# Scatter of expert outputs in tiles of 128 tokens across batch borders, with the expert outputs read back in two parts

## The reference

```python
def _L0_ffn_ref(x, gate_w, gate_b, w1, w2):
    E, H, K = 32, 2048, 8
    logits = einsum('bsd,ed->bse', x, gate_w) + gate_b
    probs = softmax(logits, axis=-2)                    # over the tokens
    vals, idx = top_k of probs per expert, K tokens     # (b, K, E)
    merged = einsum('bked,bke->bed', x[idx], vals)      # one row per batch and expert
    h = gelu(einsum('bei,eih->beh', [merged, 1], w1))
    o = einsum('bej,ejo->beo', [h, 1], w2)              # one row of 512 per batch and expert
    out = zeros_like(x).at[b, idx].add(o * vals)        # scatter back to the picked tokens

x = x + _L0_attn_ref(_layernorm(x), ...)
x = x + _L0_xattn_ref(_layernorm(x), ctx_512, ...)
x = x + _L0_ffn_ref(_layernorm(x), ...)
```

## Time and profile before

| What | Value |
|---|---|
| Median of 3 runs | 2419.74 us (2414.06 to 2422.43) |
| The profiled execution's own time | 2416.22 us |
| Its span in the trace | 2414.6 us |
| PE busy | 1965.3 us, 81% of the span |
| DVE, ACT, POOL busy | 974.0, 753.5 and 826.0 us |
| HBM read, written | 306.39 MB, 16.15 MB |

### The profile page before, as it was taken

The page is one execution under the profiler, slowest core; times in us unless marked ns, Lnnn a source line. Parts: engine busy times, 40 slices in busy tenths (PEclk is TensorE's granted clock), DMA queues, the critical chain, the costliest instruction groups (busy, mean ns, idle before and its releaser), DMA issues. The chain is left out here.

```text
span 2414.6 us, 39997 instructions
## 1 busy us (share of the span) xinstructions
PE 1965.3 (81%) x11970; PEld 1156.2 (48%) x11970; DVE 974.0 (40%) x2477; ACT 753.5 (31%) x1551; POOL 826.0 (34%) x592
## 2 busy tenths in 40 slices
PE   7789999999999999999999999986765565565533
PEld 5465666666666666666666666653211111111101
DVE  1354655656556555465555565642100000000003
ACT  2143434435444444344443444433100000000000
POOL 0244555545455455545454554553000000000000
PEclk9899999999999999999999999987877777778765
DMA  5233223233232332422323324263799999999974
GB/s 156 59 77 94 73 78 86 72 98 75 70 91 69 80 84 70 102 56 76 85 75 93 75 70 98 65 212 137 314 419 423 420 419 422 421 422 420 420 238 134
DMA packets 135414, 419.34 MB, mean 174 GB/s; under 512 B 32612, under 2 KB 74820, under 8 KB 110804
## 3 DMA queue, kind: packets, MB, share of 16 engines
q1 hardware_dynamic: 130292, 410.08, 50.0%
q10 hardware_dynamic: 4096, 7.80, 1.0%
q0 software_dynamic: 992, 1.02, 0.1%
HBM read 306.39 MB, written 16.15 MB: 134 GB/s over the span
## 5 line engine op out<-in xcount | busy, mean ns | idle before, releaser
L1035 DVE TENSOR_REDUCE maxes<-bank 112x1 f32<-112x376 f32 (+1 forms) x1024 | 508.4, 537 | 221.2 <-PE bank L1240 220.6
L863 ACT ACTIVATE probs<-bank 125x448 f32<-125x448 f32 x768 | 400.8, 546 | 355.5 <-PE bank L1262 350.1
L1262 PE MATMUL bank<-q_st,k_st 98*125 98x224 f32 x1536 | 388.0, 343 | 10.1 <-DMA q_st<-max_lo 5.5
L739 POOL TENSOR_TENSOR psum_keys<-psum_keys,probs 125x896 f32<-125x896 f32 x128 | 268.8, 2100 | 300.2 <-ACT probs L863 290.7
L1600 PE MATMUL bank<-ring,hid_T 128*32 128x512 f32 x1024 | 179.3, 864 | 207.6 <-DMA ring<-in_L_ffn_w 202.7
L1240 PE MATMUL bank<-k_st,q_st 96*112 96x376 f32 (+1 forms) x1024 | 324.1, 371 | 16.1 <-DVE maxes L1035 7.6
L1262 PEld LDWEIGHTS bank<-q_st,k_st 98*125 98x125 f32 x1536 | 270.9, 195 | 120.0 <-issue 71.5
L742 POOL TENSOR_TENSOR psum_keys<-psum_keys,probs 125x896 f32<-125x896 f32 x128 | 267.3, 2088 | 10.0
L1515 DVE TENSOR_TENSOR o_fin<-bank,b_row 16x512 f32<-16x512 f32 x32 | 21.7, 679 | 591.3 <-PE bank L1558 591.3
L1438 POOL DMA_DIRECT2D o_rows<-o_fin x31 | 15.3, 492 | 597.7 <-DVE o_fin L1515 597.7
L1240 PEld LDWEIGHTS bank<-k_st,q_st 96*112 96x112 f32 x1024 | 166.8, 183 | 75.2 <-DVE maxes L1035 39.3
(11 more groups left out here) (149 smaller groups left out, 2271.1 us busy)
## 6 DMA issues: line engine op xcount, KB each, us to landing
ring<-in_L_ffn_w SPq DMA_DIRECT2D x128, 2048.0 KB, 30.7
k_st<-k_hi SPq DMA_DIRECT2D x512, 93.8 KB, 2.2
k_st<-k_lo SPq DMA_DIRECT2D x256, 93.8 KB, 2.2
q_st<-q_hi SPq DMA_DIRECT2D x512, 28.0 KB, 1.8
ctx_nat<-in_ctx SPq DMA_DIRECT2D x16, 750.0 KB
x_in<-in_x SPq DMA_DIRECT2D x16, 448.0 KB, 3.5
q_st<-q_lo SPq DMA_DIRECT2D x256, 28.0 KB, 1.9
out<-x SPq DMA_DIRECT2D x16, 448.0 KB, 7.5
```

What stands on the lines that cost most here:

```text
L739: nc.gpsimd.tensor_tensor(psum_keys[:], psum_keys[:], lo, ALU.add).then_inc(pool_chain, 1)
L863: nc.scalar.activation(probs[n % 2][:, j, :], bank[5 + u % 2][0:SK, 0:2 * T], ACT.Exp, scale=SCALE).then_inc(probs_ready, 1)
L1035: nc.vector.tensor_reduce(maxes[:, j, t, c:c + 1], bank[2 + n % 3][0:TT, 0:SC[c + 1] - SC[c]], AX.X, ALU.max).then_inc(s_drained, 1)
L1262: last = nc.tensor.matmul(bank[5 + u % 2][0:SK, kk * T:(kk + 1) * T], k_st[slot][:, j, k * SK:(k + 1) * SK], q_st[slot][:, j, :], start=Tr ...
```

## The change

Three edits, all in the third part.

1. The x of all 3584 tokens is handled as 28 tiles of 128 consecutive tokens, whatever batch they are in. They are loaded by four DMAs of 8, 8, 8 and 4 tiles (a partition gets one token's 2 KiB of each tile), and stored one tile at a time, 28 stores of 128 partitions with 2 KiB each.
2. Four batches are seven tiles, so the scatter runs in four cycles of seven tiles. A tile that lies over a batch border gets its PSUM bank from the matmuls of two batches, each for its own partitions; a piece that doesn't fit the array's column groups of 32, 64 or 128 is split in two. This gives 12 matmuls in a cycle. VectorE takes the tiles in the order 0, 2, 4, 6, 1, 3, 5.
3. The expert rows are read back in two parts: experts 0 to 15 by four DMAs ahead of the loads of x, experts 16 to 30 by four DMAs where all were read before.

```diff
-        def fin(b):
-            return ring[0:TT, b // RW, b % RW * 2 * D:(b % RW + 1) * 2 * D].rearrange(
-                "p (t n) -> p t n", t=2)
+        NT = B * T // P
+        PER = 2 * H // D
+        rows_out = out.rearrange("b t d -> (b t) d").rearrange("(k p) d -> p k d", p=P)
+        def fin(k):
+            return ring[:, k // PER, k % PER * D:(k % PER + 1) * D]
+        CYCLE = RW * T // P
+        TURN = [0, 2, 4, 6, 1, 3, 5]
+        def drained(k):
+            return k // CYCLE * CYCLE + TURN.index(k % CYCLE) + 1
+        def tile_at(n):
+            return n // CYCLE * CYCLE + TURN[n % CYCLE]
...
                 weights(end, 1, False, (0, 1))
-                for b in range(B):
-                    if b % RW == 0:
-                        sp.wait_ge(h_full if b < B // 2 else o_full, E - 1)
-                    sp.dma_start(fin(b), out[b, :, :].rearrange("(p t) d -> p t d", p=TT)
-                                 ).then_inc(fin_loaded[b // RW], 16)
+                def read_back(r, e0, e1):
+                    sp.dma_start(o_in[r * E + e0:r * E + e1, :, :],
+                                 o_rows.rearrange("(g r) e n -> r e g n", r=RW)[r, e0:e1, :, :]
+                                 ).then_inc(o_loaded, 16)
+                sp.wait_ge(o_stored, 16 * (E - 4))
+                for r in range(RW):
+                    read_back(r, 0, E // 2)
+                for g in range(-(-NT // PER)):
+                    sp.wait_ge(h_full if g < 2 else o_full, E - 1)
+                    n = min(PER, NT - g * PER)
+                    sp.dma_start(ring[:, g, 0:n * D].rearrange("p (k d) -> p k d", d=D),
+                                 rows_out[:, g * PER:g * PER + n, :]).then_inc(fin_loaded[g], 16)
                 weights(end, 1, False, (2, 3))
                 sp.wait_ge(o_stored, 16 * (E - 1))
                 for r in range(RW):
-                    sp.dma_start(o_in[r * E:(r + 1) * E - 1, :, :],
-                                 o_rows.rearrange("(g r) e n -> r e g n", r=RW)[r, 0:E - 1, :, :]
-                                 ).then_inc(o_loaded, 16)
+                    read_back(r, E // 2, E - 1)
...
-                for b in range(B):
-                    act.wait_ge(fin_ready, 2 * b + 2)
-                    act.dma_start(out[b, :, :].rearrange("(p t) d -> p t d", p=TT), fin(b)
-                                  ).then_inc(fin_stored, 16)
-                act.wait_ge(fin_stored, 16 * B)
+                for n in range(NT):
+                    k = tile_at(n)
+                    act.wait_ge(fin_ready, n + 1)
+                    act.dma_start(rows_out[:, k, :], fin(k)).then_inc(fin_stored, 16)
+                act.wait_ge(fin_stored, 16 * NT)
...
-                for b in range(B):
-                    g, r = b // RW, b % RW
-                    if r == 0:
-                        dve.wait_ge(fin_loaded[g], 16 * RW)
-                    for t in range(2):
-                        dve.wait_ge(scat_full, g * 2 * RW + t * RW + r + 1)
-                        nc.vector.tensor_tensor(fin(b)[:, t, :], fin(b)[:, t, :],
-                                                bank[t * RW + r][0:TT, :], ALU.add
-                                                ).then_inc(fin_ready, 1)
+                for n in range(NT):
+                    k = tile_at(n)
+                    dve.wait_ge(fin_loaded[k // PER], 16)
+                    dve.wait_ge(scat_full, n + 1)
+                    nc.vector.tensor_tensor(fin(k), fin(k), bank[k % 8][:], ALU.add
+                                            ).then_inc(fin_ready, 1)
...
-                pe.wait_ge(o_loaded, 16 * (RW + GB))
-                for g in range(GB):
-                    for t in range(2):
-                        for r in range(RW):
-                            if g:
-                                pe.wait_ge(fin_ready, (g - 1) * 2 * RW + 2 * r + t + 1)
-                            rows = slice(r * E, (r + 1) * E)
-                            nc.tensor.matmul(bank[t * RW + r][0:TT, :],
-                                             tokens(picks[rows, g, :], t), o_in[rows, g, :],
-                                             start=True, stop=True).then_inc(scat_full, 1)
+                pe.wait_ge(o_loaded, 16 * (2 * RW + GB))
+                def scatter(k, r, first, parts, new, done):
+                    k += cycle * CYCLE
+                    if new and k >= 8:
+                        pe.wait_ge(fin_ready, drained(k - 8))
+                    rows = slice(r * E, (r + 1) * E)
+                    for at, n in parts:
+                        last = nc.tensor.matmul(bank[k % 8][at:at + n, :],
+                                                picks[rows, cycle, first:first + n],
+                                                o_in[rows, cycle, :], start=True, stop=True)
+                        first += n
+                    if done:
+                        last.then_inc(scat_full, 1)
+                for cycle in range(GB):
+                    scatter(0, 0, 0, [(0, 128)], True, True)
+                    scatter(1, 1, 0, [(96, 32)], True, False)
+                    scatter(3, 2, 0, [(64, 64)], True, False)
+                    scatter(5, 3, 0, [(32, 32), (64, 64)], True, False)
+                    scatter(2, 1, 32, [(0, 128)], True, True)
+                    scatter(4, 2, 64, [(0, 128)], True, True)
+                    scatter(6, 3, 96, [(0, 128)], True, True)
+                    scatter(1, 0, 128, [(0, 64), (64, 32)], False, True)
+                    scatter(3, 1, 160, [(0, 64)], False, True)
+                    scatter(5, 2, 192, [(0, 32)], False, True)
```

## The result

The changed kernel takes 2434.44 us (median of 4 runs, 2431.54 to 2438.99) against 2418.9 us for the kernel before: a ratio of 1.0063, 95% interval 1.0041 to 1.0085. It is slower by about 15 us, where 40 us less were forecast. The profiled execution took 2431.54 us.

The account below looks back on a forecast made before the run. The last 110 us were taken as the place to gain: loads of x, a read-back on one DMA engine, then the scatter. -8.9 + 3.0 - 29.6 - 4 = -39.5 us from 2418.5 gave 2379 us, range 2368 to 2392.

Parts of the forecast that it names:

- D: Scatter's start to the span's end: 26.7 us instead of 30.4, about -4 us, bounds -1 to -6.5.
- TensorE at half clock with VectorE waiting for it in each cycle (D gone): Sign in the changed profile's scatter that would show the forecast wrong, with the gain of D lost; no size given.
- A: Loads of x as four DMAs of 128 partitions: 372 GB/s instead of 257, -8.9 us, bounds 0 to -11.5.
- B: Read-back's first part (16 experts, 0.524 MB) ahead of the loads of x: costs its whole time, +3.0 us.
- C: From the last w2 to the scatter's start: 11.8 us instead of 41.4, -29.6 us.
- What bounds the kernel: Last 110 us: loads of x and w2 pure transfer, then the read-back on one engine, then VectorE and stores about level.
- the engine counts: DMA transfers: partitions shared out evenly among up to 16 engines, so 31 get 1, 16 get 16, 15 get 15.
- hidden either way: Read-back's second part (0.49 MB) right behind w2: 1.3 us or 4.1, within the 7.8 us before expert 31's rows.
- Transfers on one engine: Rival: both read-back parts stay on one DMA engine, 2407 us (2389 if only the second does); 5 in 100.
- cost by the piece: Rival: loads, stores and read-back cost by count of pieces, not bytes; sum +26 us, 2444 us; 4 in 100.
- the fixed part of a store: Rival: the scatter's 28 stores each pay 1.7 us fixed in turn; sum +9 us, 2428 us; 2 in 100.

Follow-up runs that it names:

- e1: The changed kernel with the 12 matmuls of a cycle put in order of width, VectorE's order changed to match: 2382.47 us, ratio to before 0.987.
- e2: The changed kernel in its own order, with every matmul cut into pieces of 32 columns: 2381.01 us, ratio 0.985.
- e8: The kernel of e1 with the matmuls of a cycle in pairs of one width (128, 64, 32, 128, 64, 32): 2403.82 us, ratio 0.9965.
- e4: The changed kernel with the old read-back (31 experts at once, behind the last weights): 2452.88 us, ratio 1.0145.
- e9: The kernel of e1 with SP waiting, ahead of the read-back's second part, until the last expert's w2 chunks have landed: 2371.79 us, ratio 0.9842.
- e5: The kernel of e1 with the read-back's first part (experts 0 to 15) moved behind the last weights: 2369.62 us, ratio 0.9848.

## Why the prediction was wrong

The step that failed is D, the scatter, and in it one clause: "Each row group has three per cycle, evenly, so the same packing can hold." I took 0.435 us a matmul from a stretch in which all were 32 x 112, four abreast, and multiplied it by 48 matmuls of three widths. The diff's order mixes the widths, and then they don't go abreast: from its start to the end of the span the scatter takes 2429.9 - 2350.79 = 79.1 us, where 26.7 were forecast and 30.4 measured before. e1, e2 and e8 show that the width changes are the cause. The Trainium skill ("TensorEngine Tiling (Array Packing)", Key Properties) states a rule that fits: switching the tiling mode, as against the tile, drains TensorE. The traces agree, 1.84 to 2.0 us for each group between two changes. I had not weighed that rule, and none of my rivals was this one; the closest sign I named was "TensorE at half clock with VectorE waiting for it in each cycle (D gone)", and I gave it no price. The rest of the sum holds up: sorted by width (e1), the kernel takes 2382.47 us, inside the range of 2368 to 2392, though partly because A's error and D's make up for B's. (The middle of 2416.2 and 2419.7 is 2418.0, not 2418.5; that changes nothing.)

With that, the difference of the two profiled executions adds up from intervals of before, after and e4:

| Term | Forecast, us | Measured, us | From |
|---|---|---|---|
| Before this stretch | 0 | -1.5 | expert 30's w2 stage, 2290.88 against 2292.41 |
| A, loads of 128 partitions | -8.9 | -11.4 | e4's interval against before's |
| B, narrow read-back and the stream | +3.0 | +9.1 | the interval after against e4's |
| C, last w2 to scatter | -29.6 | -29.5 | 11.9 against 41.4 |
| D, scatter to the end | -4 | +48.7 | 79.1 against 30.4 |
| Sum | -39.5 | +15.4 | spans: 2429.9 - 2414.6 = 15.3 |

**What bounds the kernel, and the engine counts: right.** The last 110 us were the place. The read-back on one engine was worth 29.5 us. 16 and 15 partitions spread over the engines: the DMA share is 1.04 in the first part (2299 to 2303) and 1.00 in the second (e9, 2328 to 2330), no longer 0.07.

**A: right, a little small.** The loads ran at 392 GB/s, over the 372 of the row taken: 18.7 us instead of 28.6, so 9.9 saved. The other 1.5 us of e4's 11.4 no run places.

**B: mechanism right, size off by a factor of three.** I took the middle of 1.4 and 4.4 us, the upper bound being the 125-partition row at 119 GB/s. Sixteen partitions then moved 115 to 134 GB/s in e5, e9 and after, which is chance: that row had five engines busy (share 0.34), these had all (1.0). With no row on so few partitions, the upper end was the value to take. The first part costs about 5 us (e9's 44.3 against e4's 38.9). The further 4 us lie in a step of C that I had costed at nothing: "hidden either way". The second part is behind w2 in the queue and yet slows it (e9). By the Trainium skill ("SBUF — State Buffer", The DMA port swizzle), DMA bandwidth depends on how many of 16 SBUF ports the partitions reach; partitions 0 to 15 reach 4. The measured 115 to 134 is 0.26 to 0.31 of the 435 that wide transfers reach here, so the rows agree. A contention in those ports would also explain the slowed w2, since part of w2 goes through the same ports; no run here shows the ports, so that stays an inference.

**C: right.** Four issues of 0.50 to 0.60 us and 1.78 us for the last to land.

**D without the width changes: right.** In e1 the scatter takes 2378.6 - 2354.34 = 24.3 us to the end of the span, 6.1 less than before, near the end of the bounds of -1 to -6.5, with stores of 128 partitions at 380 GB/s where I took 340, and with TensorE's clock at 1.00 where I had reckoned with half.

**The rivals.** Transfers on one engine, cost by the piece and the fixed part of a store are all out: the share of 1.0 in both parts contradicts the first, the loads at 392 GB/s in pieces of 2 KiB and the stores at 380 in e1 the two slower ones. That the kernel came out slower lends them nothing.

## What to carry to other kernels

Before matmuls are recounted, look at the shapes in the order in which they are issued: small matmuls go side by side in the array only among equals, so that sorting the same work by width, or cutting it all to one width, took some 55 us off this scatter. In these traces a DMA got its engines from how its number of partitions divides, and its rate also from how many partitions it reached; one transfer of 128 partitions beat two of 16 and 15, and a narrow one is not free even behind the transfer that one waits for. When an edit joins several changes, price each against rows of its own shape, and keep as the bound the row that differs most where no row has that shape.

## What the runs showed of the hardware that was not expected

- TensorE's clock. In the changed scatter and in e8 PE shows busy nearly throughout (75.6 of 76 us, 48 of 48) and yet the granted clock is 0.50 from first to last, with one to three matmuls abreast. In e1, with four abreast, it rises to 1.00 about 4 us in. A group takes 1.9 us at the lower level and about 1 us at the upper one. How much of the 57 us between the two scatters (75.8 less 18.7) is the clock's depends on the order of counting. As estimates from these numbers, 40 groups at the upper level would take some 40 us, 36 less; 12 groups at the lower level would take some 23 us, so that the sorting alone is worth some 53 us and the clock, with VectorE then the limit, the last 4. No run separated the two.
- A width change between two matmuls costs their overlap, about 1.9 us a group at 1.2 GHz, whether a group has one, two, three or (e1's first) four matmuls in it.
- Sixteen DMA engines that all show busy (share 1.0) can move anything from 115 to 435 GB/s here. The share alone doesn't tell that a stream is at its limit.
